# Adding gathered source rows on TensorE, with weighted sums, cell sums and fold streaming 128 columns

## The chip, the cores and the metric

The kernel runs on one core of one Trainium2 chip. The metric is the device time of one execution in microseconds. The engines are PE (TensorE), DVE (VectorE), ACT (ScalarE), POOL (GpSimd) and SP (SyncE, which here issues most of the DMAs). A chip core has 16 DMA engines.

## The reference

Two graph layers run over 6250 nodes with 128 features and 200000 edges, which come sorted by their destination `dst`.

- Layer 0 takes the mean of the edges' own 128 features over each destination, puts the node's features, this mean and a global vector through one product with `W`, applies softplus, adds the result to `x` and normalizes each row.
- Layer 1 makes `h = relu(ln(x @ W1 + b1))`. Each edge gets `w = sigmoid(relu(h[src] @ We1[:128] + h[dst] @ We1[128:] + be1) @ We2 + be2)`, and `aggr[dst] += w * h[src]`. A gate of `h` and `aggr` mixes the two; two normalizations and the residual with `x` follow.

The change lies in layer 1's work on the edges: in the sum of the source's and the destination's product inside the relu, and in the sum of `w * h[src]` over destinations.

## The kernel before, in words

**Layer 0 and the tables.** The edges are cut into 391 chunks of 512 (128 partitions by J = 4). Up to about 340 us the kernel streams the edge features and sums them over windows of 64 destinations by products with one-hot matrices (`edge_sums`, line 535). Then it makes the node rows, `h`, and two tables in DRAM: `src_table` holds for each node `h @ We1[:128]` (128 f32 columns, the source part) and `h` (128 more), and `dst_table` the destination part, split into three bf16 parts.

**Two ways for layer 1's edges.** The last 297 chunks are gathered: the edge loop goes over them in 149 steps `q` of two chunks. The first 94 chunks, whose destinations are low and crowded, are instead sorted by source block on DVE, ACT and PE during the same steps (`sort_rows`, line 1913, 10 tokens a step in the first class and 3 in the others, in 16 and 26 + 26 + 23 steps), and then handled by 124 "riders". A rider is attached to one of the steps, with four columns of 128 cells each.

**One chunk of the edge loop.** POOL issues four indirect DMAs (line 981), each of which brings for 128 edges the 256 columns of their source rows into one of ten gather buffers; a step has eight of them. SP loads a window of `dst_table`. DVE makes a transposed one-hot of the destinations (line 1953). PE multiplies it with the window (`dst_part`, line 564, bf16, four products a chunk) into a PSUM bank, which then holds the destination part of the 512 edges. DVE adds the gathered source part to it in PSUM (`add_src_part`, line 569, one operation for both chunks of a step), drains, takes relu and the product with `We2` in one operation (line 574) and sums it to one logit an edge (line 576). ACT applies the sigmoid. DVE makes the weighted one-hot of 40 destinations (`weigh`, line 580), and PE multiplies the gathered rows of `h` as the weights with it as the moving operand (`weighted_sums`, line 585, four f32 products a chunk of 40 columns). DVE adds the result to `aggr` at the window's place (line 589).

**One rider.** PE brings source and destination parts to its cells (lines 1467 and 1468, four f32 products each, 128 columns). DVE makes its logits (574, 576) and its placing matrix (`cell_weigh`, line 1963). PE sums weights by cell (`cell_sums_mm`, line 1489, four products of `span(u)` columns, 64, 80, 112 or 128 by class), ACT copies them, and two steps later PE multiplies them with the blocks' rows of `h` (`fold`, line 1497, the same number of columns). DVE adds that to `aggr`.

**Order.** There is no scheduler: `run_stages` writes for each engine, turn by turn, the stages with their lags, and each engine runs them in that order.

- PE: in turn t `hidden_mm(t-1)`, `wsum(t-4)`, `rider_mm(t-1)`. In `wsum` the order is fold, cell sums, weighted sums, and the signal stands on the last product.
- DVE: in turn t `hot_t(t)`, `weigh_(t-3)`, `logits(t-2)`, `acc2(t-5)`. `logits(q)` waits for `hidden(q)` from PE and for the gathers of step q.
- POOL: the eight gathers of step q, behind a wait for `wsum(q-5)`, which frees their buffers.
- ACT: `edge_weight(q)`, `sums_out`, `place_sources`, `cell_hots`, `sort_columns`.

`hidden_mm(q)` waits for `hot_t(q)` and for `logit(q-2)`, whose PSUM banks it takes over; `wsum(q)` waits for `weigh(q)` and `acc2(q-2)`. In the records each f32 product is two matmul instructions, called halves here, and each bf16 product one.

Of the kernel before, what the change touches and what calls it, by code (L numbers as in the profile page):

```python
# [17 lines left out]
ALU = mybir.AluOpType  # L18
# [25 lines left out]
def gnn_pair(nc, n_nodes, n_edges, io):  # L44
# [46 lines left out]
    with ctx:  # L91
# [92 lines left out]
        far_onehot3 = sb("far_onehot3", [P, J, WP], BF16)  # L184
# [4 lines left out]
        weighted = sb("weighted", [P, 3, 2, J, W])  # L189

        assert 2 * n_blocks <= P and P <= 2 * J * W
        count_rows = weighted[0:2 * n_blocks, 0, :, :, :].rearrange("p c j w -> p (c j w)")[:, 0:P]
# [76 lines left out]
        def gathered_pair(q):  # L269

            i = 2 * q % G_SLOTS
            n = len(pair_chunks(q)) * SLOT
            late = i - own_slots - RING_GATHERS
            if late >= 0:
                a = late_gathers[:, late * SLOT:late * SLOT + n]
            elif i >= own_slots:
                a = ring[:, ring_slots[i - own_slots]:ring_slots[i - own_slots] + n]
            else:
                a = x_rows_flat[:, i * SLOT:i * SLOT + n]
            return a.rearrange("p (j f) -> p j f", f=2 * P)  # L280


# [69 lines left out]
        PLACES = len(place_dst)  # L352
        U_SLOTS, BLOCKS = 3, COLS // min(cap for _, _, cap in CLASSES)
# [286 lines left out]
        def window_out(i):  # L640
            return sums_bank(i // 2)[:, i % 2 * W0:i % 2 * W0 + W]
# [215 lines left out]
        def _(eng):  # L857
# [6 lines left out]
            eng.memset(shift[:, :], 0.0)  # L864
            eng.iota(iota_i[:, :], pattern=[[1, W], [0, PARTS]], base=0, channel_multiplier=0)
# [425 lines left out]
        def _(eng):  # L1291
# [192 lines left out]
            def cell_sums_mm(u, q):  # L1484

                need(eng, "place_src", u)
                cap = CLASSES[riders_of[u][0]][2]
                for i in range(rider_cols(u)):
                    eng.matmul(weight_out(q, col_block(u, i))[:, 0:span(u)], place_src[:, u % 2, i, :], place_dst[u % PLACES][:, i, 0:span(u)],  # L1489
                               start=(i % cap == 0), stop=(i % cap == cap - 1), skip_group_check=True)  # L1490

            def fold(u, q):
                k, blocks = riders_of[u]
                eng.wait_ge(h_in[u % U_SLOTS], 16 * (u // U_SLOTS + 1))
                eng.wait_ge(done("pair_weight"), u + 1)
                for i, b in enumerate(blocks):
                    eng.matmul(folded_out(q)[:, 0:span(u)], h_part[:, u % U_SLOTS, i, :], pair_weight[u % 2][i][:, 0:span(u)],  # L1497
                               start=(i == 0), stop=(b == blocks[-1]), skip_group_check=True)

            def wsum(q):  # L1500
                need(eng, "weigh", q)
                need(eng, "acc2", q - 2)
                if q in folded:
                    fold(folded[q], q)
                if q in riders:
                    cell_sums_mm(riders[q], q)
                for c in pair_chunks(q):
                    last = weighted_sums(eng, window_out(c), gathered(c), weighted[:, q % 3, c % 2, :, :])
                last.then_inc(done("wsum"), 1)

            run_stages(n_steps, [(1, hidden_mm), (4, wsum), (1, rider_mm)])

            def far(item, c, start, first):
# [4 lines left out]
                dst_part(eng, hidden(0), onehot3_t[:, 0, 0, :, :], window[0:WP, 0, :]).then_inc(done("far_hidden"), 1)  # L1518
                eng.wait_ge(done("far_weigh"), item)
                weighted_sums(eng, window_out(0), gathered(0), weighted[:, 0, 0, :, :]).then_inc(done("far_wsum"), 1)  # L1520
# [21 lines left out]
        def _(eng):  # L1542
# [20 lines left out]
            last.then_inc(done("extent"), 1)  # L1563
            eng.wait_ge(done("extent"), 1)
# [401 lines left out]
            def logits(q):  # L1966
# [5 lines left out]
                need(eng, "hidden", q)  # L1972
                for j in range(2):
                    eng.wait_ge(gather_in[q % (G_SLOTS // 2)][j], 32 * sum(len(pair_chunks(i)) for i in range(q % (G_SLOTS // 2), q + 1, G_SLOTS // 2)))
                n = len(pair_chunks(q))
                add_src_part(eng, hidden_pair(q), gathered_pair(q))
                need(eng, "weight", q - 4)
                eng.drain()  # L1978
                edge_dots(eng, logit[:, q % 4, 0:n, :].rearrange("p c j -> p (c j)"), hidden_pair(q)).then_inc(done("logit"), 1)

            def weigh_(q):
# [6 lines left out]
                for k in range(len(pair_chunks(q))):  # L1988
                    last = weigh(eng, weighted[:, q % 3, k, :, :], lane_dst[:, c + k, :], weight[:, q % 4, k, :])
# [25 lines left out]
            def far(item, c, start, first):  # L2015
# [5 lines left out]
                eng.wait_ge(done("far_gather"), item * (16 * J))  # L2021
                add_src_part(eng, hidden(0), gathered(0))
                eng.drain()
                edge_dots(eng, logit[:, 0, 0, :], hidden(0)).then_inc(done("far_logit"), 1)
                eng.wait_ge(done("far_weight"), item)
                weigh(eng, weighted[:, 0, 0, :, :], far_dst[:, :], weight[:, 0, 0, :]).then_inc(done("far_weigh"), 1)
# [88 lines left out]
```

## Time and profile before

| | us |
|---|---|
| median of 3 timed runs | 2142.13 |
| lowest and highest of them | 2141.02, 2144.42 |
| the profiled execution, span from first to last instruction | 2383.5 |
| of it PE busy | 1765.2 (74%) |
| of it DVE busy | 1849.8 (78%) |
| of it POOL busy | 1410.9 (59%) |
| of it ACT busy | 1086.9 (46%) |

The profiled execution is a separate run; its own time is known here as its span alone, which is 241 us above the timed median. Shares and waits below are of that execution. PE's busy time counts matmuls whose ends are modelled, so it is no measure of how full the array is. Its mean granted clock is 0.700, where 1.0 stands for 2.4 GHz and 0.5 for 1.2 GHz.

### The profile page before, as it was taken

How to read it: one execution, taken by the hardware profiler on the slowest of the kernel's cores; microseconds unless marked ns; L12 is line 12 of the kernel's file. 1: busy time of each engine (PE TensorE's matmuls, PEld its weight loads, DVE VectorE, ACT ScalarE, POOL GpSimd, SP SyncE). 2: the span in 40 equal slices, each digit the busy share in tenths (PEclk: the TensorE clock that was granted, in tenths of full speed). 3: DMA queues.
4: the chain of work that ended last, by engine and by line, in shares of the span. 5: the costliest groups of instructions: out<-in, count | busy, mean ns of one | idle time of the engine just before them, and what ended most of it. 6: DMA issues, size and time to landing. Idle time of an engine off the chain costs nothing.

```text
span 2383.5 us, 40155 instructions
## 1 busy us (share of the span) xinstructions
PE 1765.2 (74%) x12318; PEld 1600.5 (67%) x12319; DVE 1849.8 (78%) x5049; ACT 1086.9 (46%) x2658; POOL 1410.9 (59%) x1430
## 2 busy tenths in 40 slices
PE   4999986725654577878877878878877788777790
PEld 3787875525554576767777777777777787777760
DVE  7788777738986688887888877888887777777766
ACT  2566655635531244443444444454444433444325
POOL 4555303763666666666666666666666666666635
PEclk9999996966665567576667665666676656666665
DMA  7899991353444455545454555555555555555401
GB/s 274 293 331 327 332 305 41 118 179 91 124 121 135 118 154 145 152 145 157 144 154 146 155 152 162 161 163 153 154 165 163 160 155 161 162 159 156 141 24 54
DMA packets 278498, 392.59 MB, mean 165 GB/s; under 512 B 74753, under 2 KB 178436, under 8 KB 278155
## 3 DMA queue, kind: packets, MB, share of 16 engines
q1 hardware_dynamic: 218783, 230.00, 30.7%
q0 software_dynamic: 57024, 155.79, 22.1%
q10 hardware_dynamic: 2476, 4.22, 0.5%
q8 instruction: 100, 1.64, 0.3%
q14 instruction: 115, 0.94, 0.1%
HBM read 374.69 MB, written 15.12 MB: 164 GB/s over the span
## 4 chain that ended last, share of the span: by engine, by line
PE 59%; DVE 17%; issue 16%; DVEq 4%; another core or an unknown queue 3%; ACT 1%; DMA 0%; SPq 0%; POOL 0%; ACTq 0%; POOLq 0%
PE psum L585 13%; PE psum L535 8%; PE psum L1467 7%; PE psum L1468 7%; PE psum L1489 6%; PE psum L564 4%; DVE sums L1913 3%; PE psum L1497 3%; DVE weighted L580 3%; DVE psum L574 2%; PE psum L1446 2%; PE psum L1354 2%; DVEq L1978 2%; DVE logit L576 1%
## 5 line engine op out<-in xcount | busy, mean ns | idle before, releaser
L981 POOL DMA_INDIRECT x_rows<-src_table,lane_src x720 | 692.9, 962 | 397.6 <-issue 193.6
L574 DVE SCALAR_TENSOR_TENSOR psum<-psum,we_all 128x1024 f32<-128x1024 f32 (+1 forms) x273 | 268.9, 985 | 191.4 <-remote 116.6
L1468 PE MATMUL psum<-ring,sums 128*128 128x128 f32 x980 | 285.1, 372 | 99.0 <-issue 97.8
L589 DVE TENSOR_TENSOR sums<-sums,psum 128x128 f32 (+4 forms) x812 | 200.9, 247 | 189.7 <-issue 117.3
L1467 PE MATMUL psum<-ring,sums 128*128 128x128 f32 x980 | 294.1, 387 | 68.0 <-issue 65.6
L981 POOL DMA_INDIRECT late_gathers<-src_table,lane_src x232 | 224.5, 968 | 134.9 <-issue 61.9
L981 POOL DMA_INDIRECT ring<-src_table,lane_src x236 | 226.9, 962 | 123.0 <-issue 63.4
L1468 PEld LDWEIGHTS psum<-ring,sums 128*128 128x128 f32 x980 | 231.6, 282 | 99.0 <-issue 98.3
L576 DVE TENSOR_REDUCE logit<-psum 128x8 f32<-128x1024 f32 (+1 forms) x273 | 266.9, 978 | 21.9 <-issue 2.1
L585 PE MATMUL psum<-weighted,x_rows 128*128 128x40 f32 x1440 | 265.0, 359 | 23.2 <-issue 23.2
L585 PEld LDWEIGHTS psum<-weighted,x_rows 128*128 128x128 f32 x1440 | 264.1, 281 | 22.5 <-issue 22.5
L1467 PEld LDWEIGHTS psum<-ring,sums 128*128 128x128 f32 x980 | 230.8, 284 | 69.5 <-issue 67.0
L580 DVE TENSOR_SCALAR weighted<-iota,lane_dst,weight 128x40 f32<-128x40 f32 x1188 | 267.0, 315 | 0.0
L535 PE MATMUL psum<-ring 128*64 128x128 f32 x3128 | 221.1, 284 | 27.4 <-issue 22.3
L564 PE MATMUL psum<-ring,onehot_t 120*128 120x128 bf16 x1188 | 151.0, 275 | 116.0 <-issue 102.2
L564 PEld LDWEIGHTS psum<-ring,onehot_t 120*128 120x128 bf16 x1188 | 114.0, 126 | 160.5 <-issue 155.1
L1446 PE MATMUL psum<-sums 128*98 128x256 bf16 x532 | 127.7, 392 | 122.1 <-issue 106.6
L535 PEld LDWEIGHTS psum<-ring 128*64 128x64 f32 x3128 | 173.9, 140 | 52.1 <-issue 33.6
L1446 PEld LDWEIGHTS psum<-sums 128*98 128x98 bf16 x532 | 94.3, 185 | 154.6 <-issue 151.3
L1210 ACT ACTIVATE w_node<-psum 128x64 f32<-128x64 f32 (+3 forms) x62 | 15.2, 245 | 362.2 <-remote 362.2
L1210 ACT ACTIVATE w<-psum 128x64 f32<-128x64 f32 (+3 forms) x62 | 15.3, 246 | 351.4 <-remote 350.1
L1229 ACT ACTIVATE sums<-sums 128x128 f32<-128x128 f32 x490 | 155.5, 395 | 11.5 <-remote 11.5
(263 smaller groups left out, 3680.4 us busy)
## 6 DMA issues: line engine op xcount, KB each, us to landing
ring<-in_edge_attr SPq DMA_DIRECT2D x195, 512.0 KB, 5.3
ring<-rel_table SPq DMA_DIRECT2D x74, 512.0 KB
ring<-cell_table SPq DMA_DIRECT2D x121, 256.0 KB
ring<-src_table SPq DMA_DIRECT2D x144, 128.0 KB
x_rows<-src_table,lane_src POOLq DMA_INDIRECT x720
ring<-dst_table SPq DMA_DIRECT2D x297, 32.0 KB
ring<-src_table SPq DMA_DIRECT2D x104, 64.0 KB
src_table<-ring SPq DMA_DIRECT2D x12, 512.0 KB, 2.9
```

Of the source, the lines that this page charges most:

```text
L535: last = eng.matmul(out, hot[:, j, :], v[:, j, :], start=(j == 0), stop=(j == J - 1), skip_group_check=True)
L564: last = eng.matmul(out[:, j, :], hot_t[:, j, :], win, start=True, stop=True, skip_group_check=True)
L574: eng.scalar_tensor_tensor(hid, hid, 0.0, wide["we2"][:, :].unsqueeze(1).to_broadcast([P, n, P]), ALU.max, ALU.mult)
L576: return eng.tensor_reduce(out, hid, AX.X, ALU.add)
L580: last = eng.tensor_scalar(out[:, j, :], iota1[:, 0:W], dst[:, j:j + 1], wt[:, j:j + 1], ALU.is_equal, ALU.mult)
L585: last = eng.matmul(out, rows_[:, j, P:2 * P], hot[:, j, :], start=(j == 0), stop=(j == J - 1))
L589: return eng.tensor_tensor(table[..., bass.ds(start, width)], table[..., bass.ds(start, width)], part, ALU.add)
L981: eng.indirect_dma_start(gathered(c)[:, j, :], None, src_table, bass.IndirectOffsetOnAxis(ap=lane_src[:, t:t + 1], axis=0)).then_inc(gathe ...
L1229: eng.activation(place_src[:, u % 2, i, :], iota_s, ACT.Abs, bias=cell[:, 0, at_ + i:at_ + i + 1], scale=-1.0)
L1446: eng.matmul(cell_sums(i), cols_[:, j, i * TURN:(i + 1) * TURN], rows_[:, j, :, :].rearrange("p v r -> p (v r)"), start=(t == first and i ...
L1467: eng.matmul(o, node_hot[:, u % 2, 0, e], src_part[:, u % U_SLOTS, col_block(u, i), :], start=True, stop=False, skip_group_check=True)
L1468: last = eng.matmul(o, node_hot[:, u % 2, 1, e], base_dst[:, k % 2, :], start=False, stop=True, skip_group_check=True)
```

## The change

1. **Source part on PE.** `dst_part` now opens an accumulation in the bank with its first product and leaves it open. A new PE stage `hidden_sum(q)`, at the end of turn q + 1, waits for the gathers of step q and adds the source part by four f32 products a chunk: the weights are the identity, the moving operand is the gathered rows' first 128 columns. `logits(q)` on DVE waits for `hidden_sum(q)` instead of `hidden(q)` and the gathers; its addition and its drain are gone. The same is done in `far`, which handles chunks wider than a window.
2. **128 columns in the weighted sums.** The moving operand begins at the chunk's 40 columns and runs on over its neighbours, to 128; the buffer is longer by 88 columns, which are filled with zeros once. The result's further columns fall on places in the bank that are written later or not read. The chunks' places in the bank are 40 apart instead of 64.
3. **128 columns in cell sums and fold**, instead of `span(u)`.
4. **Order in `wsum`:** weighted sums, fold, cell sums; the signal is on the last of them.
5. Around these: `far_onehot3` shares the last placing buffer, POOL fills that buffer and the 88 columns once at the start, and DVE uses one semaphore less for `extent`.

```diff
         def dst_part(eng, out, hot_t, win):
             for j in range(J):
-                last = eng.matmul(out[:, j, :], hot_t[:, j, :], win, start=True, stop=True, skip_group_check=True)
+                last = eng.matmul(out[:, j, :], hot_t[:, j, :], win, start=(j == 0), stop=False, skip_group_check=True)
             return last
         def add_src_part(eng, out, rows_):
-            return eng.tensor_tensor(out, out, rows_[:, :, 0:P], ALU.add)
+            for j in range(J):
+                last = eng.matmul(out[:, j, :], ident[:, :], rows_[:, j, 0:P], start=False, stop=True, skip_group_check=True)
+            return last
...
-        weighted = sb("weighted", [P, 3, 2, J, W])
+        STREAM = P
+        weighted = sb("weighted", [P, 3, 2 * J * W + STREAM - W])
...
+        def weighted_stream(s, c, j):
+            at_ = (c * J + j) * W
+            return weighted[:, s, at_:at_ + STREAM]
...
-        def weighted_sums(eng, out, rows_, hot):
+        def weighted_sums(eng, out, rows_, s, c):
             for j in range(J):
-                last = eng.matmul(out, rows_[:, j, P:2 * P], hot[:, j, :], start=(j == 0), stop=(j == J - 1))
+                last = eng.matmul(out, rows_[:, j, P:2 * P], weighted_stream(s, c, j), start=(j == 0), stop=(j == J - 1), skip_group_check=True)
             return last
...
         def window_out(i):
-            return sums_bank(i // 2)[:, i % 2 * W0:i % 2 * W0 + W]
+            return sums_bank(i // 2)[:, i % 2 * W:i % 2 * W + W]
+        def window_stream(i):
+            return sums_bank(i // 2)[:, i % 2 * W:i % 2 * W + STREAM]
...
+            eng.memset(weighted[:, :, 2 * J * W:], 0.0)
+            eng.memset(place_dst[PLACES - 1][:, :, :], 0.0)
...
-                    eng.matmul(weight_out(q, col_block(u, i))[:, 0:span(u)], place_src[:, u % 2, i, :], place_dst[u % PLACES][:, i, 0:span(u)],
-                               start=(i % cap == 0), stop=(i % cap == cap - 1), skip_group_check=True)
+                    last = eng.matmul(weight_out(q, col_block(u, i)), place_src[:, u % 2, i, :], place_dst[u % PLACES][:, i, :],
+                                      start=(i % cap == 0), stop=(i % cap == cap - 1), skip_group_check=True)
...
-                    eng.matmul(folded_out(q)[:, 0:span(u)], h_part[:, u % U_SLOTS, i, :], pair_weight[u % 2][i][:, 0:span(u)],
-                               start=(i == 0), stop=(b == blocks[-1]), skip_group_check=True)
+                    last = eng.matmul(folded_out(q), h_part[:, u % U_SLOTS, i, :], pair_weight[u % 2][i][:, :],
+                                      start=(i == 0), stop=(b == blocks[-1]), skip_group_check=True)
...
             def wsum(q):
                 need(eng, "weigh", q)
                 need(eng, "acc2", q - 2)
+                for c in pair_chunks(q):
+                    last = weighted_sums(eng, window_stream(c), gathered(c), q % 3, c % 2)
                 if q in folded:
-                    fold(folded[q], q)
+                    last = fold(folded[q], q)
                 if q in riders:
-                    cell_sums_mm(riders[q], q)
-                for c in pair_chunks(q):
-                    last = weighted_sums(eng, window_out(c), gathered(c), weighted[:, q % 3, c % 2, :, :])
+                    last = cell_sums_mm(riders[q], q)
                 last.then_inc(done("wsum"), 1)
-            run_stages(n_steps, [(1, hidden_mm), (4, wsum), (1, rider_mm)])
+            def hidden_sum(q):
+                for j in range(2):
+                    eng.wait_ge(gather_in[q % (G_SLOTS // 2)][j], 32 * sum(len(pair_chunks(i)) for i in range(q % (G_SLOTS // 2), q + 1, G_SLOTS // 2)))
+                for c in pair_chunks(q):
+                    last = add_src_part(eng, hidden(c), gathered(c))
+                last.then_inc(done("hidden_sum"), 1)
+            run_stages(n_steps, [(1, hidden_mm), (4, wsum), (1, rider_mm), (1, hidden_sum)])
...
             def logits(q):
-                need(eng, "hidden", q)
-                for j in range(2):
-                    eng.wait_ge(gather_in[q % (G_SLOTS // 2)][j], 32 * sum(len(pair_chunks(i)) for i in range(q % (G_SLOTS // 2), q + 1, G_SLOTS // 2)))
+                need(eng, "hidden_sum", q)
                 n = len(pair_chunks(q))
-                add_src_part(eng, hidden_pair(q), gathered_pair(q))
                 need(eng, "weight", q - 4)
-                eng.drain()
                 edge_dots(eng, logit[:, q % 4, 0:n, :].rearrange("p c j -> p (c j)"), hidden_pair(q)).then_inc(done("logit"), 1)
```

## Rows read from the trace of the kernel before

Times are microseconds from the start of the span unless a column says ns. In the stage table each engine has its busy time and, in brackets, its number of instructions; behind them stand the granted clock of PE, the DMA engines' busy share and GB/s. A row of the chain has start, length and the group. A timeline row has start, busy time, engine, line, operation, the tiles and the count; square brackets hold the idle time before it and its releaser. A row of the groups has busy time and mean ns, then idle time before and releasers.

**Rows 1.** Stage table: busy time of each engine, granted clock, DMA.

```profile
0.00:340.00 340.00, 289.18 (x3967) 242.96 (x3970) 266.46 (x638) 180.99 (x644) 152.29 (x148) 0.97 0.90 309
...
740.00:2273.00 1533.00, 1189.87 (x6588) 1114.39 (x6587) 1203.09 (x3099) 671.32 (x1472) 989.25 (x1028) 0.65 0.52 153
```

**Rows 2.** The chain that ended last: shares, then pieces of 1206 to 1226 us.

```profile
PE 59%; DVE 17%; issue 16%; DVEq 4%; another core or an unknown queue 3%; ACT 1%; DMA 0%; SPq 0%; POOL 0%; ACTq 0%; POOLq 0%
...
1206.58 0.45 PE psum L564 x8
1207.03 0.22 PE psum L1497 x2
1207.25 0.89 PE psum L1489 x8
1208.14 1.77 PE psum L585 x16
...
1210.21 0.22 PE psum L1468 x2
...
1222.02 3.37 PE psum L585 x16
...
1225.97 0.43 PE psum L1468 x2
```

**Rows 3.** Groups on POOL in the edge loop, with their waits.

```profile
L981 POOL DMA_INDIRECT x_rows<-src_table,lane_src x720 | 692.9, 962 | 397.6 <-issue 193.6 <-remote 171.6 <-PE psum L585 30.2
L981 POOL DMA_INDIRECT ring<-src_table,lane_src x236 | 226.9, 962 | 123.0 <-issue 63.4 <-remote 58.2 <-PE psum L585 1.4
L981 POOL DMA_INDIRECT late_gathers<-src_table,lane_src x232 | 224.5, 968 | 134.9 <-issue 61.9 <-remote 60.6 <-DMA dst_table<-late_gathers 12.4
```

**Rows 4.** Timeline of POOL: gathers at the loop's start and in its middle.

```profile
565.19 0.95 POOL L981 DMA_INDIRECT x_rows<-src_table,lane_src  x1 [25.48 <-PE psum L585]
...
1218.59 0.95 POOL L981 DMA_INDIRECT x_rows<-src_table,lane_src  x1 [1.84 <-remote]
1219.84 0.95 POOL L981 DMA_INDIRECT x_rows<-src_table,lane_src  x1 [0.30 <-issue]
```

**Rows 5.** Timeline of DVE in three kinds of steps.

```profile
643.01 0.47 DVE L1953 TENSOR_SCALAR onehot_t<-ring,row_node 120x1024 bf16<-120x1024 bf16 x1
...
654.06 0.47 DVE L1953 TENSOR_SCALAR onehot_t<-ring,row_node 120x1024 bf16<-120x1024 bf16 x1
...
1206.68 0.70 DVE L574 SCALAR_TENSOR_TENSOR psum<-psum,we_all 128x512 f32<-128x512 f32 x1 [1.41 <-remote]
...
1208.06 1.22 DVE L569 TENSOR_TENSOR psum<-psum,x_rows 128x1024 f32<-128x1024 f32 x1
1209.36 1.23 DVE L574 SCALAR_TENSOR_TENSOR psum<-psum,we_all 128x1024 f32<-128x1024 f32 x1
...
1215.49 1.78 DVE L580 TENSOR_SCALAR weighted<-iota,lane_dst,weight 128x40 f32<-128x40 f32 x8
...
1948.07 0.70 DVE L574 SCALAR_TENSOR_TENSOR psum<-psum,we_all 128x512 f32<-128x512 f32 x1 [2.42 <-remote]
...
1955.76 1.76 DVE L580 TENSOR_SCALAR weighted<-iota,lane_dst,weight 128x40 f32<-128x40 f32 x8
```

**Rows 6.** Group of VectorE's addition that reads the first gather buffers.

```profile
L569 DVE TENSOR_TENSOR psum<-psum,x_rows 128x1024 f32<-128x1024 f32 x90 | 110.1, 1223 | 0.0
```

**Rows 7.** Stage table of three short stretches of one step.

```profile
1221.40:1224.80 3.40, 3.40 (x18) 3.40 (x18) 2.93 (x6) 2.85 (x7) 2.54 (x3) 0.50 0.98 267
1224.80:1228.20 3.40, 3.40 (x17) 3.40 (x18) 3.40 (x16) 0.00 (x0) 2.74 (x3) 0.50 0.56 180
1228.20:1231.60 3.40, 2.21 (x21) 1.77 (x20) 1.93 (x7) 1.24 (x5) 1.40 (x2) 0.99 0.23 73
```

**Rows 8.** Timeline of POOL: a fill at the kernel's start.

```profile
4.81 5.37 POOL L879 MEMSET sums<- 128x6336 f32 x1
```

More of the change, by code:

```diff
@@ L188, in gnn_pair, with weighted_hot @@
         weight = sb("weight", [P, 4, 3, J])
-        weighted = sb("weighted", [P, 3, 2, J, W])
+        STREAM = P
+        weighted = sb("weighted", [P, 3, 2 * J * W + STREAM - W])
+        def weighted_hot(s, c):
+            return weighted[:, s, c * J * W:(c + 1) * J * W].rearrange("p (j w) -> p j w", j=J)
+        def weighted_stream(s, c, j):
+            at_ = (c * J + j) * W
+            return weighted[:, s, at_:at_ + STREAM]
         assert 2 * n_blocks <= P and P <= 2 * J * W
-        count_rows = weighted[0:2 * n_blocks, 0, :, :, :].rearrange("p c j w -> p (c j w)")[:, 0:P]
+        count_rows = weighted[0:2 * n_blocks, 0, 0:P]
         pad_rows = sb("pad_rows", [(dst_rows - padded) * PARTS, P], BF16)
@@ L1517, in far @@
                 eng.wait_ge(done("far_window"), item * 16)
-                dst_part(eng, hidden(0), onehot3_t[:, 0, 0, :, :], window[0:WP, 0, :]).then_inc(done("far_hidden"), 1)
+                dst_part(eng, hidden(0), onehot3_t[:, 0, 0, :, :], window[0:WP, 0, :])
+                eng.wait_ge(done("far_gather"), item * (16 * J))
+                add_src_part(eng, hidden(0), gathered(0)).then_inc(done("far_hidden"), 1)
                 eng.wait_ge(done("far_weigh"), item)
-                weighted_sums(eng, window_out(0), gathered(0), weighted[:, 0, 0, :, :]).then_inc(done("far_wsum"), 1)
+                weighted_sums(eng, window_stream(0), gathered(0), 0, 0).then_inc(done("far_wsum"), 1)
             further_windows(eng, 1, far)
@@ L1562, in _ @@
                     last = eng.tensor_reduce(extent[0:n, g, k:k + 1], chunk_dst[0:n, g, :], AX.X, op)
-            last.then_inc(done("extent"), 1)
-            eng.wait_ge(done("extent"), 1)
+            step(last)
             eng.wait_ge(done("constants"), 1)
@@ L1988, in weigh_ @@
                 for k in range(len(pair_chunks(q))):
-                    last = weigh(eng, weighted[:, q % 3, k, :, :], lane_dst[:, c + k, :], weight[:, q % 4, k, :])
+                    last = weigh(eng, weighted_hot(q % 3, k), lane_dst[:, c + k, :], weight[:, q % 4, k, :])
                 last.then_inc(done("weigh"), 1)
@@ L2020, in far @@
                 eng.wait_ge(done("far_hidden"), item)
-                eng.wait_ge(done("far_gather"), item * (16 * J))
-                add_src_part(eng, hidden(0), gathered(0))
-                eng.drain()
                 edge_dots(eng, logit[:, 0, 0, :], hidden(0)).then_inc(done("far_logit"), 1)
                 eng.wait_ge(done("far_weight"), item)
-                weigh(eng, weighted[:, 0, 0, :, :], far_dst[:, :], weight[:, 0, 0, :]).then_inc(done("far_weigh"), 1)
+                weigh(eng, weighted_hot(0, 0), far_dst[:, :], weight[:, 0, 0, :]).then_inc(done("far_weigh"), 1)
                 eng.wait_ge(done("far_wsum"), item)
```

17 lines of the change are left out of this document (4 added, 13 removed).

## The prediction, written before the changed kernel was run

> **What bounds the kernel now.** I read the stage table first [rows 1]. Up to 340 us PE runs at a granted clock of 0.97 and the DMA engines are 0.90 busy; the change does almost nothing there. Behind it runs the edge loop of 149 steps, and there no engine is full: in 740 to 2273 us PE is busy 1190 of 1533 us, DVE 1203, POOL 989, at a granted clock of 0.65. So the question is which wait ends last in one step.
>
> The chain that ended last puts 59% on PE, 17% on DVE and 16% on "issue", PE standing between two matmuls for nothing that the profile shows [rows 2]. Taken alone this says that PE is the bound. But the timed median is 2142.1 us and this span is 2383.5: the recorded execution holds 241 us that timed runs don't. Where they sit shows on POOL. Its gathers start 1.25 us apart, and only the first of each eight waits for others, 1.84 us in the rows shown [rows 4]. Over the loop, POOL is busy 692.9 + 226.9 + 224.5 = 1144.3 us, idle 193.6 + 63.4 + 61.9 = 318.9 us by "issue", and idle 655.5 - 318.9 = 336.6 us for others [rows 3]. Without any wait for others the span would be 2383.5 - 336.6 = 2046.9 us. Of the waits, 12.4 us for a landing [rows 3] and 25.5 us for the first weighted sum [rows 4] are the start of the loop and stay in any run, 38 us together. That gives 2085 us as a floor for POOL's durations. The median lies 57 us above it. So I read timed runs as going mostly at POOL's pace: 1144.3/1188 = 0.963 us busy and 0.30 us issue, 1.265 us a gather, 10.1 us a step.
>
> **What makes the 57 us?** DVE, I think. In a step with three sorted tokens and a rider its work runs without a gap of waiting from 1206.68 to 1215.49 + 1.78 = 1217.27 us: 10.6 us. In the first class of the sort (ten tokens, no rider) from 643.01 to 654.06 us: 11.05 us. Without sorting, from 1948.07 to 1957.52 us: 9.45 us [rows 5]. The code has 16 steps of the second kind and 26 + 26 + 23 = 75 of the first. Against POOL's 10.1 us they run over by 16 x 0.95 = 15 us and 75 x 0.5 = 38 us, 53 us together; the other steps are shorter than POOL's and can't give it back, since POOL is then the slower one. 53 against 57 us is the agreement on which the forecast rests. PE needs less: at the high clock the chain has 0.89 us for eight halves of the cell sums, 1.77 for sixteen halves of the weighted sums, 0.22 for two of the rider's halves (1.77 for sixteen) [rows 2]; 0.45 for the destination part and 0.22 for the fold; the sort's three, which I put in at 0.11 each, make it 5.4 us in all. The low clock doubles nearly every term, which gives 10.4 us. At the mean of 0.65 it is 5.4/0.65 = 8.3 us, under 10.1.
>
> **The change, part by part.** (1) *VectorE's addition goes.* Its start-to-start distance to the next operation, drain included, is 1209.36 - 1208.06 = 1.30 us [rows 5]; a row of these has a mean of 1.22 us busy [rows 6]. The three kinds of steps become 9.75, 9.3 and 8.15 us. All are under POOL's 10.1 us, so of the 149 x 1.30 = 194 us only the 53 us that stand over POOL's pace can come off the time; the rest becomes DVE idle time.
> (2) *TensorE's addition comes:* 4 f32 products a chunk, 8 a step, each in two halves, 128 columns on a 128x128 weight. The row of the same form is the rider's: 0.22 us a product at the high clock, 0.43 at the low [rows 2], so 1.8 or 3.4 us a step. PE's step becomes 7.2 us at high, 13.8 at low. To stay under 10.1 us it needs a mean granted clock of 7.2/10.1 = 0.71. If it gets that, the cost is nothing and POOL's pace covers it; without that cover see the rivals.
> (3) *The wider streams.* The weighted sums move 128 instead of 40 columns, cell sums and fold 128 instead of 64 to 112. Sixteen halves of 40 columns took 1.77 us high and 3.37 low, 0.11 and 0.21 each; two halves of 128 columns took 0.22 and 0.43, the same each [rows 2]. So I take widening at zero. FP8 and Floating Point Precision in the Trainium skill (TensorE Precision Notes) says true FP32 takes four passes through the array; by passes of moving columns alone a product of 40 columns would be less than a third of one of 128, and the widening would add over 1 us to a step's sums. The rows disagree for 40 columns, and the measured pace decides.
> (4) *The clock.* In 1221.4 to 1224.8 us PE is busy throughout at 0.50 with the 40-column sums, and the clock stays low; in 1224.8 to 1228.2 us it streams 128-column products, and the next stretch has 0.99 [rows 7]. In the first stage, where the heavy f32 work moves 128 columns, it is 0.97 [rows 1]. After the change all f32 streams of a step are 128 wide, so I expect the high level behind the first full stretch of a step and a mean of 0.8 to 0.9. TensorE: Matmul & The Clock Gate in the Trainium skill (Part 1) says that the gate follows how busy the engine has been; by how busy it is alone the rise should have come behind 1221.4 to 1224.8 us and widening would change nothing. Here the row speaks for the wider streams. What is left between 0.65 and 0.85 is what pays for part 2: 7.2/0.85 = 8.5 us a step.
> (5) *The wait moves.* Before, DVE waited for the gathers, at its step q + 2. Now PE waits for them at the end of its step q + 1, with the next destination part and the next weighted sums queued behind, and POOL waits for the weighted sums five steps back. That costs one of three steps of slack between landing and use; two steps, 20 us, remain for it. DVE's dots now wait for the end of a whole PE step; late next is DVE by that, which has about 1 us a step to spare after part 1. I take zero, with 0 to 0.3 us a step (45 us) as bounds: below, nothing excludes a small gain from DVE no longer standing on the gathers; above, 0.3 is one issue gap.
> (6) *The order.* Sums go before fold and cell sums; the signal still stands on the last of them, so POOL gets it at the same place. The two new fills on POOL are 512 + 3 x 88 columns; 6336 columns took 5.37 us [rows 8], so about 0.7 us before 340 us of DMA-bound work: nothing to 0.7.
> I give 14 us back for steps that PE does at the low clock: 15 of 149 steps, each 13.8 - 10.1 = 3.7 us too long, a quarter of it not hidden by the slots. The share is my choice.
> Sum: 2142.1 - 53 + 14 = 2103 us. Against the profiled execution the same 53 us come off a span of 2383.5, if its extra waits stay; they need not. The runs agree within 0.2%, about 4 us, and that is what I count as no change.
>
> **Rivals.** *POOL is already the pace everywhere (0.12).* Then DVE's work is shorter in timed runs than here, and the 57 us are waits of the start. For it: only an account of two sums that agree stands against it. Time 2142 us.
> *DVE is the pace everywhere (0.14).* Then POOL's 1.265 us would be stretched by the recording, as PE is. The whole 194 us would come off: 1948 us; half of it 2045. Against: a gather's 0.95 us are the same at 565 us, when the loop has hardly begun, and at 1219 us [rows 4].
> *PE becomes the pace (0.16), slower than before.* If the clock stays at 0.65, PE's step takes 7.2/0.65 = 11.1 us, 1.0 over POOL's, in the 124 steps with a rider: 2085 + 124 = 2209 us. It decides below a mean of 0.71. Against: rows 7; for: PE will now stand at the end of each step for gathers, and no row isolates what the clock does behind such a stand.
> *The widening isn't free (0.04), slower.* At the rider's 0.43 us for 128 columns, 88 columns more are 0.30 us low or 0.15 high a product; with cell sums some 1.6 us high a step: 8.8/0.85 = 10.4 us, 0.3 over POOL's, 2103 + 45 = 2148 us, and far more if the clock stays low. Against: part 3. By the four passes of the Trainium skill's FP8 and Floating Point Precision (TensorE Precision Notes) the number would be of the same size; the rows of 40 columns speak against it.
>
> **How the numbers follow.** Forecast 0.54 (2103 us, from 2085 to about 2137), 0.14 and 0.12 and 0.16 and 0.04 as above. Faster 0.54 + 0.14 = 0.68; within 0.2% 0.12; slower 0.16 + 0.04 = 0.20. The range of 2040 to 2170 takes the forecast, no change, the milder half of the DVE rival and the milder part of the two slow ones; the forecast's own range is 2085 to 2137, which is the bound of part 5 and the 14 us taken whole or not.
>
> **What would show it.** Right: the addition's rows (line 569) are gone and DVE's busy time falls by about 180 us; sixteen new matmul halves a step at 0.11 us; the weighted sums still at 0.11 and 0.21 us a half; granted clock of the loop from 0.65 to over 0.8; POOL's waits shorter than 336.6 us, above all in the first sixteen steps. Wrong: a clock near 0.65 with PE busy over 0.9 of the loop (PE is the pace); or POOL's gathers at another distance in a run at 1948 us; or DVE standing several us a step for the new sum.

## The result, and the profile after

The changed kernel takes 2087.72 us (median of 4 runs, 2087.17 to 2088.43), the kernel before beside it 2141.77 us (2141.02 to 2144.42). The ratio is 0.9745, 95% interval 0.9734 to 0.9757: 54 us less. The profiled execution took 2087.29 us with a span of 2085.6, so this time the profile is of an execution like the timed ones.

The page of the changed kernel: span, busy time by engine, the granted clock in 40 slices, shares of the chain that ended last, and five groups.

```profile
span 2085.6 us, 44756 instructions
...
PE 1617.8 (78%) x14694; PEld 1509.3 (72%) x14695; DVE 1663.6 (80%) x4900; ACT 1086.7 (52%) x2658; POOL 1411.1 (68%) x1432
...
PEclk9999999698888789999899999899999898999995
...
POOL 45%; PE 21%; issue 17%; DVE 11%; DMA 3%; DVEq 1%; ACT 1%; SPq 0%; ACTq 0%; POOLq 0%
...
L983 POOL DMA_INDIRECT x_rows<-src_table,lane_src x720 | 695.8, 966 | 227.3 <-issue 215.5
L570 DVE SCALAR_TENSOR_TENSOR psum<-psum,we_all 128x1024 f32<-128x1024 f32 (+1 forms) x273 | 271.1, 993 | 145.7 <-PE psum L564 145.2
L564 PE MATMUL psum<-x_rows,ident 128*128 128x128 f32 x1440 | 224.4, 321 | 163.5 <-DMA x_rows<-src_table,lane_src 163.5
...
L983 POOL DMA_INDIRECT ring<-src_table,lane_src x236 | 226.0, 958 | 71.9 <-issue 71.6
...
L983 POOL DMA_INDIRECT late_gathers<-src_table,lane_src x232 | 221.8, 956 | 70.7 <-issue 70.1
```

Against [rows 2, 3]: PE's share of the chain goes from 59% to 21%, POOL's from 0 to 45%. (The recording before is the one that lies 241 us over its timed runs; repeated, below, it has PE at 18%.) Of POOL's idle time before its gathers, 227.3 + 71.9 + 70.7 = 369.9 us, all but 12.7 us is its own "issue". VectorE's addition is gone (busy time 1849.8 to 1663.6 us), and line 564, now the identity products, stands for gathers that have not landed, with DVE behind it. Timeline of the changed kernel's PE, in two steps of the loop:

```profile
1299.70 2.02 PE L564 MATMUL psum<-late_gathers,ident 128*128 128x128 f32 x16 [3.31 <-DMA late_gathers<-src_table,lane_src]
1301.56 0.25 PE L1454 MATMUL psum<-ident_b,ring 98*128 98x98 bf16 x2
...
1302.09 2.00 PE L581 MATMUL psum<-weighted,x_rows 128*128 128x128 f32 x16
1303.93 0.39 PE L1500 MATMUL psum<-w_node,ring 128*128 128x128 f32 x2
...
1306.84 0.39 PE L1470 MATMUL psum<-ring,sums 128*128 128x128 f32 x2
...
1319.64 3.75 PE L564 MATMUL psum<-x_rows,ident 128*128 128x128 f32 x16 [3.18 <-DMA x_rows<-src_table,lane_src]
1323.18 1.06 PE L558 MATMUL psum<-ring,onehot_t 120*128 120x128 bf16 x8
```

Sixteen halves of identity products take 1301.56 - 1299.70 = 1.86 us at 2.4 GHz and 1323.18 - 1319.64 = 3.54 at 1.2 GHz. The weighted sums, now 128 columns wide, take 1303.93 - 1302.09 = 1.84. Then, twice in 20 us, PE stands over 3 us for a gather. POOL has no such hole; its timeline in the same stretch:

```profile
1318.66 0.95 POOL L983 DMA_INDIRECT x_rows<-src_table,lane_src  x1 [0.30 <-issue]
1319.91 0.94 POOL L983 DMA_INDIRECT x_rows<-src_table,lane_src  x1 [0.30 <-issue]
1321.16 0.95 POOL L983 DMA_INDIRECT x_rows<-src_table,lane_src  x1 [0.30 <-issue]
```

### The profile page after: what moved, and what is told of

It is laid out like the page before. It is cut to its first block, busy times and chain, and to the rows that moved or that the text cites. A ratio compares the mean times of both kernels' runs of the same rounds, so it can differ in the third digit from the quotient of the medians.

```text
span 2085.6 us, 44756 instructions
## 1 busy us (share of the span) xinstructions
PE 1617.8 (78%) x14694; PEld 1509.3 (72%) x14695; DVE 1663.6 (80%) x4900; ACT 1086.7 (52%) x2658; POOL 1411.1 (68%) x1432
## 4 chain that ended last, share of the span: by engine, by line
POOL 45%; PE 21%; issue 17%; DVE 11%; DMA 3%; DVEq 1%; ACT 1%; SPq 0%; ACTq 0%; POOLq 0%
POOL x_rows L983 27%; PE psum L529 10%; POOL ring L983 9%; POOL late_gathers L983 8%; DVE sums L1925 3%; PE psum L1356 2%; PE psum L564 2%; DVE stats L1837 1%; PE psum L581 1%; PE psum L537 1%; DVE weighted L576 1%; DMA x_rows<-src_table,lane_src 1%; DVE ring L1849 1%; DVE psum L570 1%; PE psum L1386 1%
## 5 line engine op out<-in xcount | busy, mean ns | idle before, releaser
L983 POOL DMA_INDIRECT x_rows<-src_table,lane_src x720 | 695.8, 966 | 227.3 <-issue 215.5
L570 DVE SCALAR_TENSOR_TENSOR psum<-psum,we_all 128x1024 f32<-128x1024 f32 (+1 forms) x273 | 271.1, 993 | 145.7 <-PE psum L564 145.2
L1193 ACT ACTIVATE weight<-logit,be_all 128x12 f32<-128x12 f32 (+2 forms) x149 | 45.2, 303 | 622.7 <-DVE logit L572 622.7
L564 PE MATMUL psum<-x_rows,ident 128*128 128x128 f32 x1440 | 224.4, 321 | 163.5 <-DMA x_rows<-src_table,lane_src 163.5
L564 PEld LDWEIGHTS psum<-x_rows,ident 128*128 128x128 f32 x1440 | 209.1, 231 | 173.9 <-issue 142.5
L983 POOL DMA_INDIRECT ring<-src_table,lane_src x236 | 226.0, 958 | 71.9 <-issue 71.6
L983 POOL DMA_INDIRECT late_gathers<-src_table,lane_src x232 | 221.8, 956 | 70.7 <-issue 70.1
L1469 PE MATMUL psum<-ring,sums 128*128 128x128 f32 x980 | 190.4, 276 | 1.3 <-DVE logit L572 1.3
L1470 PE MATMUL psum<-ring,sums 128*128 128x128 f32 x980 | 189.5, 275 | 0.0
L581 PE MATMUL psum<-weighted,x_rows 128*128 128x128 f32 x1440 | 188.0, 285 | 1.5 <-DVE sums L585 1.5
L581 PEld LDWEIGHTS psum<-weighted,x_rows 128*128 128x128 f32 x1440 | 176.5, 200 | 1.8 <-issue 1.8
L1469 PEld LDWEIGHTS psum<-ring,sums 128*128 128x128 f32 x980 | 148.7, 192 | 2.5 <-DVE logit L572 2.2
L1470 PEld LDWEIGHTS psum<-ring,sums 128*128 128x128 f32 x980 | 148.8, 192 | 0.0
L1223 ACT ACTIVATE sums<-sums,ones 128x1024 f32<-128x1024 f32 (+1 forms) x124 | 141.3, 1140 | 9.1 <-issue 0.7
L1221 ACT ACTIVATE sums<-ring,sums 128x1024 f32<-128x1024 bf16 (+1 forms) x124 | 139.4, 1124 | 2.0 <-PE psum L1470 2.0
L1083 ACT ACTIVATE ring<-psum 128x128 f32<-128x128 f32 x196 | 53.1, 271 | 141.4 <-PE psum L537 141.2
```

Source lines behind the costliest of these rows:

```text
L564: last = eng.matmul(out[:, j, :], ident[:, :], rows_[:, j, 0:P], start=False, stop=True, skip_group_check=True)
L570: eng.scalar_tensor_tensor(hid, hid, 0.0, wide["we2"][:, :].unsqueeze(1).to_broadcast([P, n, P]), ALU.max, ALU.mult)
L581: last = eng.matmul(out, rows_[:, j, P:2 * P], weighted_stream(s, c, j), start=(j == 0), stop=(j == J - 1), skip_group_check=True)
L983: eng.indirect_dma_start(gathered(c)[:, j, :], None, src_table, bass.IndirectOffsetOnAxis(ap=lane_src[:, t:t + 1], axis=0)).then_inc(gathe ...
L1223: eng.activation(hots, hots, ACT.Relu, bias=ones[:, 0:1], scale=-1.0).then_inc(done("cell_hot"), 1)
L1469: eng.matmul(o, node_hot[:, u % 2, 0, e], src_part[:, u % U_SLOTS, col_block(u, i), :], start=True, stop=False, skip_group_check=True)
```

## The experiments

Behind the result come four sets of runs, each set on another chip. Each time stands against the kernel before on the same chip in the same set.

### The kernel before again

No edit.

> The kernel before, unchanged, to see whether its profiled execution is again 2383 us long where timed runs take 2142. If the 241 us are a disturbance of one recording, span near 2142 and POOL's waits for others under 100 us instead of 336.6. If the recording always slows this kernel, span near 2383 again, with the same 1.2 us gaps between matmuls on PE. Time 2142 in both cases.

Measured: 2141.77 us, span 2140.1, mean granted clock 0.759. The 241 us of the first recording are absent. Its page (shares of the chain, POOL's first group) and who held POOL up in 470 to 2100 us (total us, times, longest):

```profile
DVE 47%; DVEq 20%; PE 18%; issue 8%; POOL 3%; DMA 1%; ACT 1%; SPq 0%; ACTq 0%; POOLq 0%
...
L981 POOL DMA_INDIRECT x_rows<-src_table,lane_src x720 | 689.9, 958 | 261.1 <-issue 211.2
```

```profile
POOL x_rows L981 <- PE psum L585: 47.3, 26, 8.8
...
POOL ring L981 <- PE psum L585: 15.9, 9, 3.5
POOL late_gathers L981 <- PE psum L585: 15.5, 10, 4.3
```

The chain is DVE's, not PE's as in [rows 2]. POOL waits 47.3 + 15.9 + 15.5 = 78.7 us for weighted sums, and PE, which makes them, stands for DVE's logits (same view, PE's rows):

```profile
PE psum L1467 <- DVE logit L576: 160.0, 87, 3.4
...
PE psum L564 <- DVE logit L576: 35.0, 23, 2.7
```

The changed kernel's rows of the same view:

```profile
POOL x_rows L983 <- PE psum L581: 7.6, 5, 5.5
POOL x_rows L983 <- PE psum L1491: 2.1, 7, 0.3
POOL late_gathers L983 <- PE psum L1491: 0.6, 2, 0.3
POOL ring L983 <- PE psum L1491: 0.3, 1, 0.3
```

10.6 us are left, so 68 went. POOL's own busy time and "issue" grew from 1486.9 to 1500.8 us (part of it because the short waits just counted hide an issue gap), and 68 - 14 = 54 us is the gain. Its place is seen with stage tables of this run and of the changed kernel, cut where POOL starts the gathers of steps 5, 17, 48, 79, 107 and 148. Columns as in [rows 1]; first the kernel before:

```profile
533.20:672.07 138.87, 80.87 (x528) 77.36 (x528) 128.54 (x403) 66.54 (x140) 92.21 (x97) 0.66 0.41 120
672.07:988.20 316.13, 228.42 (x1409) 216.34 (x1409) 282.45 (x748) 142.00 (x313) 238.98 (x248) 0.68 0.57 164
988.20:1322.46 334.26, 261.68 (x1632) 248.17 (x1633) 302.65 (x811) 173.65 (x383) 237.93 (x249) 0.71 0.58 169
1322.46:1617.57 295.11, 238.33 (x1511) 227.01 (x1510) 268.93 (x722) 157.37 (x365) 213.85 (x224) 0.71 0.61 178
1617.57:2033.03 415.46, 324.40 (x2175) 309.21 (x2176) 374.56 (x900) 192.98 (x423) 311.65 (x328) 0.76 0.64 187
```

and the changed kernel:

```profile
532.47:655.70 123.23, 92.01 (x723) 88.57 (x722) 113.45 (x391) 66.54 (x140) 93.04 (x97) 0.85 0.46 134
655.70:971.81 316.11, 240.90 (x1957) 235.14 (x1956) 255.84 (x739) 147.56 (x322) 240.53 (x249) 0.89 0.57 168
971.81:1287.14 315.33, 257.69 (x2159) 252.26 (x2157) 265.09 (x786) 178.02 (x392) 239.76 (x248) 0.92 0.61 178
1287.14:1569.91 282.77, 230.48 (x1960) 225.41 (x1960) 239.72 (x703) 160.18 (x369) 214.49 (x225) 0.93 0.65 189
1569.91:1981.39 411.48, 331.09 (x2752) 324.67 (x2752) 309.67 (x824) 188.56 (x402) 311.52 (x328) 0.90 0.63 185
```

The third number is the length. The five stretches, of 12, 31, 31, 28 and 41 steps, became shorter by 15.6, 0.0, 18.9, 12.3 and 4.0 us, and the five steps ahead of them by 3.2 (533.20 - 472.12 before, 532.47 - 474.56 after, from POOL's timeline). That is 54 us. DVE's busy time (the third engine column) per step was 10.7, 9.1, 9.8, 9.6 and 9.1 us, and most of the time came off where it was high. A step of POOL's own takes 10.1 us, and after the change all but the first class of the sort lie within 0.1 us of it (316.11/31 = 10.20, 10.17, 10.10, 10.04; the first 10.27).

### VectorE's addition left out, nothing put in its place

```diff
-                add_src_part(eng, hidden_pair(q), gathered_pair(q))
                 need(eng, "weight", q - 4)
-                eng.drain()
```

> The kernel before with the addition of the source part left out (with its drain), so that the logits lack the source part; all other work is there and PE's work is as before. Theory A: 2085 to 2092 us, as the changed kernel, since POOL's pace is reached either way. Theory B (PE's clock): 2135 to 2142 us, since PE's work is as before.

Measured: 2089.46 us (2088.43 to 2092.69), ratio 0.9762 (0.9737 to 0.9786); chain POOL 44%, PE 21%, issue 18%, DVE 12%. With the old widths, the old order and no products on PE the time is 2 us above the changed kernel's result and 4 us above that of its second set (2085.38 us, below). This is the main reading: the gain is what DVE no longer does, and the products on PE cost nothing that can be measured. The clock was no condition for it either; the stage table of this run in 740 to 1975 us:

```profile
740.00:1975.00 1235.00, 963.05 (x6416) 924.95 (x6416) 1007.49 (x2863) 643.99 (x1435) 936.69 (x978) 0.75 0.63 182
```

POOL is as busy as after the change (936.69 against 937.38 us) at a granted clock of 0.75.

### Only the products, at the old widths

```diff
-                last = eng.matmul(out, rows_[:, j, P:2 * P], weighted_stream(s, c, j), start=(j == 0), stop=(j == J - 1), skip_group_check=True)
+                last = eng.matmul(out, rows_[:, j, P:2 * P], weighted_stream(s, c, j)[:, 0:W], start=(j == 0), stop=(j == J - 1), skip_group_check=True)
```

and cell sums and fold at `span(u)` columns again.

> The change with the old widths: the addition is on TensorE by 128-column products, weighted sums move 40 columns, cell sums and fold 64 to 128. Theory A: DVE is relieved and the new products' own stream is 128 wide; 2088 to 2105 us, if the mean granted clock in the loop is over 0.71. Theory B or the rival 'PE becomes the pace': clock near 0.65 to 0.7 and 2150 to 2210 us.

Measured: 2090.8 us (2089.56 to 2091.62), ratio 0.9762 (0.9739 to 0.9785), chain POOL 47%. The new order of `wsum` is in this kernel too. The wide streams are worth 3 to 5 us by this (2090.8 against 2087.7 and, in its second set, 2085.4), from different sets of runs whose ratios overlap within their intervals. Its stage table of 740 to 1975 us, and from the timeline its weighted sums of 40 columns:

```profile
740.00:1975.00 1235.00, 995.54 (x8368) 975.96 (x8369) 1007.62 (x2868) 654.07 (x1439) 937.18 (x978) 0.92 0.63 183
```

```profile
1303.87 1.93 PE L581 MATMUL psum<-weighted,x_rows 128*128 128x40 f32 x16
1305.63 0.43 PE L1500 MATMUL psum<-w_node,ring 128*128 128x80 f32 x2
```

Sixteen halves take 1.76 us from start to start, against 1.84 with 128 columns: the widening costs 0.08 us, which POOL's pace covers. And the clock is 0.92 without it.

### Only the wide streams and the order; addition on VectorE

The changed kernel with `add_src_part` back on DVE, `dst_part` closed again and `hidden_sum` taken out of PE's stages.

```diff
-            run_stages(n_steps, [(1, hidden_mm), (4, wsum), (1, rider_mm), (1, hidden_sum)])
+            run_stages(n_steps, [(1, hidden_mm), (4, wsum), (1, rider_mm)])
...
+                dve_add_src(eng, hidden_pair(q), gathered_pair(q))
                 need(eng, "weight", q - 4)
+                eng.drain()
```

> The change with the addition left on VectorE: only the 128-column streams, their places and the order in wsum. Theory A (DVE's excess over POOL's pace in 91 steps makes the 57 us): DVE keeps its 10.6 and 11.05 us steps, so 2138 to 2142 us although the clock rises. Theory B (PE's low clock makes them): 2088 to 2100 us. A small gain with a risen clock would leave part of it with PE.

Measured: 2138.09 us (10 runs), ratio 0.9981 (0.9967 to 0.9995); chain DVE 37%, PE 18%, POOL 17%, DVEq 14%. The 4.4 us that come off (2142.46 - 2138.09; 1 to 7 by the interval) are all that the streams and the order give by themselves. Stage tables of 740 to 1975 us, the kernel before (the repeated run), then this one:

```profile
740.00:1975.00 1235.00, 965.75 (x6183) 917.80 (x6182) 1115.81 (x2900) 629.08 (x1395) 906.94 (x949) 0.73 0.61 178
```

```profile
740.00:1975.00 1235.00, 838.54 (x6179) 783.08 (x6180) 1115.23 (x2904) 630.33 (x1397) 904.77 (x949) 0.87 0.61 178
```

The wide streams, with the new order, raise the clock from 0.73 to 0.87, and PE is busy 127 us less. DVE is as busy as before, and so the time stays.

### Both additions, and the weight of PE's work

To show that DVE's 1.3 us a step make the difference also beside the products on PE, the changed kernel got VectorE's addition as well (the source part counts twice):

```diff
+                dve_add_src(eng, hidden_pair(q), gathered_pair(q))
                 need(eng, "weight", q - 4)
+                eng.drain()
```

> The changed kernel with VectorE's addition put back beside TensorE's, so that the source part is counted twice: DVE has its 1.30 us a step again, PE keeps the new products and the high clock. Theory A (DVE's excess over POOL's pace made the 57 us): 2138 to 2145 us. Theory B (the clock): 2088 to 2095 us.

Measured: 2450.64 us, ratio 1.0384 (1.0359 to 1.0409), chain PE 58%. But in this set, on another chip, the kernel before took 2357.71 us (7 runs, 2356.79 to 2361.78), 10% more than the 2142 us of the chips used so far, where the expectations' numbers come from. The run says nothing on the question it was made for. Three more kernels ran in that set. PE's addition three times:

```diff
-                for c in pair_chunks(q):
-                    last = add_src_part(eng, hidden(c), gathered(c))
+                for _ in range(3):
+                    for c in pair_chunks(q):
+                        last = add_src_part(eng, hidden(c), gathered(c))
```

> The changed kernel with TensorE's addition done three times, so the source part counts three times: 2 x 1.8 us more a step at the high clock. PE's step is 7.2 + 3.6 = 10.8 us at the high clock, over POOL's 10.1 in the 124 rider steps. If PE has the room that the prediction gave it (2.9 us a step at the high clock), 2150 to 2200 us with PE as the pace and a clock over 0.95; if PE had been near its limit already, over 2350 us.

Measured: 2966.06 us, ratio 1.2555 (1.2512 to 1.2598), chain PE 77%. Three instead of four gathers a chunk, from the eleventh gathered chunk on, in both kernels (the counts in the waits for the gathers follow):

```diff
-                for j in range(J):
+                for j in range(J if c < G_SLOTS else J - 1):
```

> The kernel before with three instead of four gathers a chunk from the eleventh gathered chunk on; the fourth quarter of each chunk uses old rows. POOL's step is 7.6 us. Theory A: DVE was the pace in the sorting steps already and now is in the others too (9.5 against 10.1 us in some 57 steps), so only 20 to 40 us come off: 2100 to 2122 us. If POOL were the pace in most of the kernel before, 150 us or more would come off.

> The changed kernel with the same three gathers a chunk. Theory A: POOL was the pace in all 149 steps, so the next slower engine sets it: DVE with about 9.75 us in 11 steps, 9.6 in 75 and 8.2 in 57, which makes 1920 to 1960 us. If some other wait holds the changed kernel at 2088 us, it stays over 2050.

Measured: the kernel before with three gathers 2158.82 us (ratio 0.9157, 0.9144 to 0.917; chain DVE 50%, DVEq 20%), the changed kernel with three 2089.19 us (ratio 0.886, 0.8847 to 0.8872; chain PE 52%). On this chip fewer gathers bring the kernel before from 2358 down to 2159 us, with DVE in front again. The expectations of these three kernels were for chips of 2142 us; only the changed kernel with three gathers was run again on one.

The next set ran on a third chip, where the kernel before took 2142.66 us (13 runs). The changed kernel once more, both additions once more, and three gathers in the changed kernel once more, with the same edits:

> The changed kernel again, beside a new set of the kernel before: one run (e_both and its neighbours) found the kernel before at 2358 us instead of 2142, on another chip. If this call lands on a chip like the first one, 2088 us against 2142. If it lands on one like the second, the PE signals that there come late until a batch of gathers is out hold POOL's step at about 11.9 us, and with PE's larger step I expect no gain: 2340 to 2420 us against 2358.

> As e_both, whose run came from a chip on which every kernel of this study is slower. Where the kernel before takes 2142 us, theory A (DVE's excess over POOL's pace) gives 2138 to 2145 us and theory B (the clock) 2088 to 2095 us. Where it takes 2358 us, about 2450 us again.

> As e_after_g3. Where the kernel before takes 2142 us, theory A gives 1920 to 1960 us, with DVE as the pace behind POOL. Where it takes 2358 us, about 2090 us again.

Measured: the change 2085.38 us (2081.19 to 2088.86), ratio 0.9736 (0.9717 to 0.9754), clock 0.904. Both additions 2145.94 us (10 runs), ratio 1.0016 (1.0007 to 1.0026); chain DVE 43%, PE 18%, DVEq 15%, POOL 10%; that is 1 us above the upper end expected. Three gathers 1935.57 us (1932.96 to 1936.08), ratio 0.9031 (0.9016 to 0.9046); chain DVE 39%, PE 24%, DVEq 23%, issue 10%.

These two close the argument from both sides. Give DVE its addition back beside the products, at a clock of 0.94 in the loop, and all 60 us return (2145.94 - 2085.38). Take a quarter of the gathers off POOL and 150 us more go (2085.38 - 1935.57), until DVE is the pace. In the kernel after, then, POOL sets the step; one engine back stands DVE, at 1936 us.

A last run was to say how much room PE has: its addition twice.

```diff
-                for c in pair_chunks(q):
-                    last = add_src_part(eng, hidden(c), gathered(c))
+                for _ in range(2):
+                    for c in pair_chunks(q):
+                        last = add_src_part(eng, hidden(c), gathered(c))
```

> The changed kernel with TensorE's addition done twice, so the source part counts twice: 1.8 us more a step at 2.4 GHz, 9.0 us in all, and the wider streams keep the clock up. Where the kernel before takes 2142 us: if PE has the room of 2.9 us a step that the prediction gave it at the high clock, 2086 to 2100 us with a granted clock of 0.93 or more in the loop; if the price of the products is already on the path, 149 x 1.8 = 268 us more, 2356 us. Where the kernel before takes 2358 us, no reading of PE's room, and well over 2450 us.

Measured: 2806.69 us, ratio 1.1778 (1.1745 to 1.1811), chain PE 74%. It fell on a fourth chip, where the kernel before took 2379.36 us (2377.14 to 2384.78), so it doesn't answer its question. How much more work PE could take at 2088 us was not measured.

## Why the prediction was right

**The floor of POOL.** Forecast 2085 us. Measured 2087.7, with POOL at its own pace from the first gather to the last but for 10.6 us of waits for PE. The mechanism was right, and the 1.25 us from gather to gather held. That the number came out so close is luck, for three errors of the working cancel. It kept 38 us of waits at the start "in any run"; the changed kernel has 12.7 us of such waits in all, 5.5 in place of the 25.5, and none for the landing that cost 12.4. It took all 336.6 us of waits out, though each of them also hides an issue gap: once the waits are gone, "issue" is 215.5 + 71.6 + 70.1 = 357.2 us and not 318.9, 38.3 more. And what lies before the first gather and behind the last was 476.7 + 109.2 us in the first recording and 474.6 + 99.5 in the changed kernel's, 11.8 less. With all three, 2046.9 + 12.7 + 38.3 - 11.8 = 2086.1 us, against a span of 2085.6. That the other 241 us were the recording's was the wrong reason: the kernel before takes that long on some chips in every run (below).

**The 57 us of DVE.** Forecast 15 us in the first class of the sort and 38 in the other three; measured 18.8 (15.6 + 3.2) and 31.2 (0.0 + 18.9 + 12.3), with 4.0 behind them: 54 for 53. The sum was right and its parts less so; that they add up is partly luck. I took one step at 1206 us, 10.6 us long, for all 75. But in 672 to 988 us DVE's busy time is 9.1 us a step against 9.8 in the next stretch, and there nothing came off; in 988 to 1322 us it was more than the 13 us expected. One difference between the two is in the repeated run's rows: DVE's placing operation (line 1963, four a rider) runs 88 times in the first and 124 in the second, so 9 of the first 31 steps have no rider, while the working gave one to each of the 75. The addition's own price held: DVE's busy time is 1842.6 us in the repeated run and 1663.6 after, 179 us less, to which the drains come (forecast 194 with them). Of that, 54 reached the time.

**PE's products.** 1.8 and 3.4 us a step forecast; 1.86 and 3.54 measured. From 1299.70 to 1306.84 + 0.39 us one PE step is 7.5 us, forecast 7.2. In 740 to 1975 us PE is busy 1000.12 of 1235 us, 8.2 us of each 10.1; forecast 8.5.

**The widening.** Zero forecast, 0.08 us a step for the weighted sums measured.

**The clock.** Forecast 0.8 to 0.9, measured 0.91 in the loop. Its cause was told half right. The wide streams (with the order) do raise it, from 0.73 to 0.87, but the products without them bring it to 0.92. TensorE: Matmul & The Clock Gate in the Trainium skill (Part 1) says that the gate follows how busy the engine has been. By busy time alone the wide kernel, 838.54 us busy, should have been granted no more than the kernel before with its 965.75. It got more, so busy time as a trace records it does not settle the clock; what does, no run here says. The condition "a mean of at least 0.71" was met with room. In the repeated run even the kernel before has 0.73 in this stretch; the 0.65 of [rows 1] is from the first recording, which looks like the second kind of chip below.

**The wait that moves.** PE stands 163.5 + 57.2 + 45.1 = 265.8 us for gathers in 470 to 2100 us and DVE 145.2 us for PE; POOL loses nothing by it. Zero was right: two steps of slots were enough. The range's upper end of about 2137 us does not follow from its terms (2089 + 45 = 2134, and 2148 with the 14 us).

**The step that was mis-sized** is the 14 us given back for steps at the low clock, a quarter of 15 x 3.7 us. The low clock comes, as at 1319.64 us behind a stand of 3.18 us (at 1299.70, behind one of 3.31, it doesn't), but POOL's gathers go on at 1.25 us through it. It is no rarer than was put in: a mean of 0.91 between the levels 0.5 and 1.0 is, as an estimate, 18% of the time at the low one, against 15 of 149 steps. Without the 14 the sum is 2089 us, against 2087.7; the slots hide all of it, not three quarters.

**The rivals.** POOL as the pace already: refuted by 78.7 us of waits. DVE as the pace everywhere: refuted, though its 1948 us is about what the changed kernel takes (1936) once POOL has three gathers. PE as the pace and a costly widening: refuted on the chips where the kernel before takes 2142 us. The changed kernel itself was not run on a chip where the kernel before takes 2358 us or more. PE's work is dear there: with its addition three times the kernel stood 608 us above the kernel before, with both additions 93. With three gathers the change was still 70 us ahead (2089.2 against 2158.8); with four this stays open, and a loss there is not excluded.

## What to carry to other kernels

When no engine is full, find the one whose period is fixed and count, class of step by class of step, how far each other engine's work runs over it: only that excess comes off, here 54 of 194 us. One step read from a trace doesn't stand for its class. When waits are taken out of an engine's idle time, put back the issue gap that each of them hides. Leaving an operation out, with nothing in its place, is the cheapest test of what moving it can bring. And when the profiled span and the timed median differ by 10%, record the kernel again before a bound is read from it: the chain named PE in one recording and DVE in the other.

## What the runs showed of the hardware

**Two kinds of chips.** The kernel before took 2142 us in the runs of the result and on two of the chips behind it, and 2358 and 2379 us on the other two, each within 0.5% over its runs. Each chip was used in one set of runs only, so that the chip itself makes the difference, and not something else about that set, is not shown. On the second kind PE stands between products of one group and nothing in the profile holds it. Timeline of PE with its addition doubled, on such a chip, and POOL's last gather of the eight with the next one:

```profile
1303.60 3.74 PE L564 MATMUL psum<-x_rows,ident 128*128 128x128 f32 x32
...
1307.95 1.16 PE L581 MATMUL psum<-weighted,ring 128*128 128x128 f32 x7
1309.55 0.60 PE L581 MATMUL psum<-weighted,ring 128*128 128x128 f32 x3 [0.45 <-issue]
1311.02 1.02 PE L581 MATMUL psum<-weighted,ring 128*128 128x128 f32 x5 [0.86 <-issue]
1312.49 0.57 PE L581 MATMUL psum<-weighted,ring 128*128 128x128 f32 x1 [0.46 <-issue]
...
1313.90 1.87 PE L1491 MATMUL psum<-sums 128*128 128x128 f32 x8 [0.33 <-issue]
```

```profile
1311.36 0.95 POOL L983 DMA_INDIRECT x_rows<-src_table,lane_src  x1 [0.30 <-issue]
1316.05 0.94 POOL L983 DMA_INDIRECT ring<-src_table,lane_src  x1 [3.75 <-PE psum L1491]
```

PE starts again every 1.47 us, and the gaps of this step end about when POOL's last gather does. A signal of PE is late meanwhile. Its identity products end at 1303.60 + 3.74 = 1307.34 us, and the operation of DVE that waits for them starts 6.6 us later, when the gaps are over. The profile calls the releaser "remote":

```profile
1313.94 1.23 DVE L570 SCALAR_TENSOR_TENSOR psum<-psum,we_all 128x1024 f32<-128x1024 f32 x1 [5.98 <-remote]
```

In the changed kernel's own profile the same two are 0.04 us apart (1299.70 + 2.02 = 1301.72 us, then 1301.76). A signal given behind the gaps isn't late on the second kind either: the sums' last product ends at 1313.90 + 1.87 = 1315.77 us, and POOL goes on at 1316.05. In the first recording PE started again every 1.43 us, and the sums' signal may have been late in the same way. Timeline of its weighted sums:

```profile
1207.98 1.93 PE L585 MATMUL psum<-weighted,x_rows 128*128 128x40 f32 x16
```

These end at 1209.91 us, and POOL goes on at 1218.59 [rows 4], 8.7 us later; 1.84 us of that is a wait, again for "remote", since the eight gathers before last until 1216.75. On a chip of the first kind the same pair of rows, PE's and POOL's of the repeated run, is 0.28 us apart (1318.63 + 3.55 = 1322.18, then 1322.46):

```profile
1318.63 3.55 PE L585 MATMUL psum<-weighted,late_gathers 128*128 128x40 f32 x16
```

```profile
1322.46 0.94 POOL L981 DMA_INDIRECT late_gathers<-src_table,lane_src  x1 [4.32 <-PE psum L585]
```

With a quarter of the gathers gone, the kernel before comes down from 2358 to 2159 us there. That doesn't make the second kind as fast as the first: the changed kernel with three gathers takes 2089 us on one and 1936 on the other, 8% more. That the gaps have to do with POOL's gathers is a reading of these rows and not shown; by what path, and why only on some chips, stays open.

**A gather's price is POOL's.** Some 0.95 us busy and 0.30 us of issue for 128 rows is the pace of this kernel, and it is the same on both kinds of chips (mean busy 962 to 968 ns in [rows 3], 956 to 966 ns after). DMA: Bandwidth & Descriptors in the Trainium skill (Anatomy of one DMA, SWDGE path) puts a DMA's fixed cost mostly on its completion and not on its setup. No run here splits the time of one DMA. Of 1188 issued one behind the other it is POOL's own 1.25 us for each that sets the time.
